# The head of a two-layer transformer kernel: tokens by lots of two tiles, query blocks by half the weights, and turns of the identity ahead

## The reference, cut to what matters

```
n  = layernorm(x)                          # x: (4, 256, 256)
q  = (n @ Wq + bq).reshape(b, 16, t, 128)  # Wq: (256, 2048)
h  = silu(n @ rw1.T + rb1)                 # router, hidden layer of 64
logits = (h @ rw2.T + rb2)[:, :16] + gates # top 2 of 16 experts, low-rank parts
```

## Time and profile before

| | us |
|---|---|
| median of 3 executions | 442.82 |
| lowest, highest | 442.76, 443.11 |
| the profiled execution, its time | 443.39 |
| its span, first to last instruction | 441.4 |
| PE busy in it | 422.6 |

### The profile page before, as it was taken

The page is one execution under the profiler, slowest core; times in us unless marked ns, Lnnn a source line. Parts: engine busy times, 40 slices in busy tenths (PEclk is TensorE's granted clock), DMA queues, the critical chain, the costliest instruction groups (busy, mean ns, idle before and its releaser), DMA issues.

```text
span 441.4 us, 8830 instructions
## 1 busy us (share of the span) xinstructions
PE 422.6 (96%) x3054; PEld 377.6 (86%) x3054; DVE 308.0 (70%) x906; ACT 245.7 (56%) x670; POOL 165.4 (37%) x293
## 2 busy tenths in 40 slices
PE   2999999899999999999999999999999989999897
PEld 1788889799999999999999999899998766577797
DVE  4645675678787888887877776657688985387442
ACT  3464563577777878786967686333314613553130
POOL 3050001455555555545555530101166005999000
PEclk9999999999999999999999999999999999999999
DMA  6920011141010100101000000000099932999002
GB/s 188 225 87 1 2 48 50 51 142 50 0 50 2 35 15 12 38 1 51 1 0 3 1 1 0 26 13 12 25 313 298 310 87 67 284 299 235 1 13 83
DMA packets 41979, 34.45 MB, mean 78 GB/s; under 512 B 6689, under 2 KB 40145, under 8 KB 41937
## 3 DMA queue, kind: packets, MB, share of 16 engines
q1 hardware_dynamic: 41552, 32.85, 26.5%
q0 software_dynamic: 384, 1.05, 0.8%
HBM read 31.80 MB, written 2.10 MB: 77 GB/s over the span
## 4 chain that ended last, share of the span: by engine, by line
PE 93%; DVE 3%; ACT 2%; issue 1%; DMA 1%; POOL 0%; DVEq 0%
PE bank L921 22%; PE bank L923 22%; PE bank L922 22%; PE bank L1079 5%; PE bank L1091 3%; PE bank L1070 3%; PE bank L1312 2%; PE bank L1279 2%; PE bank L1323 2%; PE bank L1324 2%; PE bank L1121 2%; PE bank L1299 2%; DVE GT L1787 1%; PE bank L1228 1%; DMA X<-in_L_attn_x 1%
## 5 line engine op out<-in xcount | busy, mean ns | idle before, releaser
L581 POOL TENSOR_TENSOR arena<-arena,rinv 128x384 f32<-128x384 f32 x64 | 53.0, 828 | 82.0 <-DVE rinv L1565 82.0
L921 PE MATMUL bank<-XTl,WA 128*128 128x512 f32 x128 | 54.3, 424 | 2.6 <-POOL WA L548 1.7
L923 PE MATMUL bank<-XTh,WA 128*128 128x512 f32 x128 | 51.3, 401 | 0.0
L922 PE MATMUL bank<-XTh,WA 128*128 128x512 f32 x128 | 51.3, 401 | 0.0
L746 ACT ACTIVATE PT<-bank 128x256 fp32r<-128x256 f32 x64 | 24.5, 382 | 34.1 <-PE bank L1079 34.1
L1569 DVE TENSOR_TENSOR PT<-bank,PT 128x256 fp32r<-128x256 f32 x64 | 27.2, 425 | 19.7 <-ACT arena L747 19.7
L921 PE MATMUL bank<-WA,XTh 128*128 128x256 f32 x128 | 38.4, 300 | 0.6 <-DVE K L1540 0.6
L572 POOL CAST Q<-arena 128x128 fp32r<-128x128 f32 x64 | 18.7, 292 | 48.4 <-PE bank L923 48.4
L922 PE MATMUL bank<-WA,XTl 128*128 128x256 f32 x128 | 35.7, 279 | 0.0
L923 PE MATMUL bank<-WA,XTh 128*128 128x256 f32 x128 | 35.7, 279 | 0.0
L1557 DVE CUSTOM_DVE_ANT_0 arena<-bank,posm 128x128 f32<-128x128 f32 x64 | 18.1, 282 | 20.9 <-PE bank L923 20.9
(11 more groups left out here) (327 smaller groups left out, 1449.8 us busy)
## 6 DMA issues: line engine op xcount, KB each, us to landing
arena<-in_L_ffn_Wg SPq DMA_DIRECT2D x6, 704.0 KB, 8.4
arena<-in_L_ffn_Wu SPq DMA_DIRECT2D x6, 704.0 KB, 10.5
arena<-in_L_ffn_Wd SPq DMA_DIRECT2D x6, 512.0 KB, 7.8
arena<-in_L_attn_Wq SPq DMA_DIRECT2D x4, 512.0 KB, 6.5
arena<-in_L_attn_Wk SPq DMA_DIRECT2D x8, 256.0 KB, 2.7
arena<-in_L_attn_Wv SPq DMA_DIRECT2D x8, 256.0 KB, 3.2
arena<-in_L_attn_Wo SPq DMA_DIRECT2D x1, 2048.0 KB, 8.6
arena<-in_L_ffn_Wd SPq DMA_DIRECT2D x6, 192.0 KB, 7.6
```

The lines of the kernel that those rows point to most:

```text
L581: pool.tensor_tensor(pr, pr, r[:, :, None].to_broadcast([P, 3, P]), ALU.mult).then_inc(s_p, 1)
L921: pe.matmul(dst, wh, xl, start=start, stop=False)
L922: pe.matmul(dst, wl, xh, start=False, stop=False)
L923: return pe.matmul(dst, wh, xh, start=False, stop=stop)
```

## The change

Ahead of everything PE turns the identity into bank 7, 32 times. Tokens are handled in four lots of two tiles instead of two of four: statistics, root, normalisation, turns (one bank for each lot, both halves of the features in it), high and low parts. The first two quarters of the query weights are loaded in halves and cut in halves; POOL makes both low halves of the first quarter. The first four blocks are computed by 256 tokens: `first_queries` does them for the first lot, one product of the three at a time over four banks, and `queries(0..3)` for the second lot. The blocks' order becomes that of `Q_AT`: quarter 0 half 0, quarter 1 half 0, quarter 0 half 1, quarter 1 half 1, then as before. `Q_FREE` gives the block after which a quarter's place is free. ScalarE's and VectorE's lists for the first 12 blocks are written out. The semaphores `s_wqa` and `s_w1` for the new halves are declared too.

```diff
+Q_AT = [(g, half, blk) for g, half in ((0, 0), (1, 0), (0, 1), (1, 1), (2, 0), (2, 1), (3, 0), (3, 1)) for blk in range(4)]
+Q_FREE = {2: 12, 3: 16, 4: 24, 5: 32}
+CHUNKS = 4
+WARM = 32
...
         @block.sync
         def _(sp):
-            for b in range(B):
+            def load_x(b):
                 sp.dma_start(X[:, 2 * b:2 * b + 2, :], x_t[:, b]).then_inc(s_x[b], 16)
-                if b == 1:
-                    sp.dma_start(WQv[:, 0], wq_t[:, :, 0:512]).then_inc(s_wq[0], 16)
+
+            def load_wq_halves(g):
+                for c in range(C):
+                    sp.dma_start(WQv[:, g, c], wq_t[:, c, 512 * g:512 * g + 512]).then_inc(s_wq[g] if c else s_wqa[g], 16)
+
+            load_x(0)
+            load_x(1)
+            load_wq_halves(0)
             for i, n in enumerate(("bq", "bk", "bv")):
                 sp.dma_start(VB[16 * i:16 * i + 16, :], row(a["L0_attn_" + n], H)).then_inc(s_vb, 16)
+            load_x(2)
+            load_x(3)
+            load_wq_halves(1)
             sp.dma_start(stR1, a["L0_ffn_rw1"]).then_inc(s_r, 16)
             sp.dma_start(stR2, a["L0_ffn_rw2"][0:E0, :]).then_inc(s_r, 16)
             sp.wait_ge(s_pad, 3)
             sp.dma_start(rb1c[0:HID, :], a["L0_ffn_rb1"].rearrange("(p a) -> p a", a=1)).then_inc(s_r, 16)
             sp.dma_start(rg[:, 0], a["L0_ffn_rb2"][0:E0].partition_broadcast(P)).then_inc(s_r, 16)
             sp.dma_start(rg[:, 1], a["L0_ffn_gates"].partition_broadcast(P)).then_inc(s_r, 16)
-            sp.dma_start(WQv[:, 1], wq_t[:, :, 512:1024]).then_inc(s_wq[1], 16)
             sp.dma_start(stW, two(a["L0_ffn_W"])).then_inc(s_sw, 16)
             sp.dma_start(stA, a["L0_ffn_A"].rearrange("(o e) r i -> (e r) o i", o=2)).then_inc(s_sw, 16)
...
             pool.wait_ge(s_w0, 1)
             pool.tensor_tensor(WA[:, 0, 1, 0:512], WQ[:, 0:512], WA[:, 0, 0, 0:512].bitcast(F32), ALU.subtract).then_inc(s_w0, 1)
+            pool.wait_ge(s_wh, 1)
+            pool.tensor_tensor(WA[:, 0, 1, 512:1024], WQ[:, 512:1024], WA[:, 0, 0, 512:1024].bitcast(F32), ALU.subtract).then_inc(s_wl, 1)
             pool.wait_ge(s_bo, 96)
...
-                    act.wait_ge(s_qf, 8 * (n - 1)) if n < 6 else act.wait_ge(s_kf, 8 * (n - 5))
+                    act.wait_ge(s_qf, Q_FREE[n]) if n < 6 else act.wait_ge(s_kf, 8 * (n - 5))
...
+            def deviations(i):
+                act.wait_ge(s_var, i + 1)
+                nc.scalar.activation(rstd[:, 2 * i:2 * i + 2], mv[:, 2 * i:2 * i + 2, 1], ACT.Sqrt).then_inc(s_std, 1)
+
+            def tokens_high(i):
+                act.wait_ge(s_xt, i + 1)
+                nc.scalar.activation(XTh[:, :, T * i:T * i + T], pb[4 + i][:].rearrange("p (c n) -> p c n", c=C), ACT.Copy).then_inc(s_xth, 1)
+
+            def first_high(g, c):
+                act.wait_ge(s_wq[g] if c else s_wqa[g], 16)
+                nc.scalar.activation(WA[:, g, 0, 512 * c:512 * c + 512], WQ[:, 1024 * g + 512 * c:1024 * g + 512 * c + 512],
+                                     ACT.Copy).then_inc(s_wh if c else (s_w0, s_w1)[g], 1)
...
+            deviations(0)
+            first_high(0, 0)
+            tokens_high(0)
+            deviations(1)
+            first_high(0, 1)
+            tokens_high(1)
+            first_high(1, 0)
+            deviations(2)
+            first_high(1, 1)
+            act.wait_ge(s_vc, 2)
+            q_copy(0)
+            deviations(3)
+            q_copy(2)
+            tokens_high(2)
+            q_copy(4)
+            tokens_high(3)
+            q_copy(6)
+            q_copy(8)
+            q_copy(10)
...
+            act.wait_ge(s_t, 2)
+            act.wait_ge(s_pad, 3)
+            nc.scalar.activation(R1Th[:, :, 0:HID], pb[5][:, 0:2 * HID].rearrange("p (c n) -> p c n", c=C), ACT.Copy).then_inc(s_tc, 1)
+            nc.scalar.activation(R2T[0:HID, :], pb[5][0:HID, 256:256 + E0], ACT.Copy).then_inc(s_tc, 1)
+            for g in range(1, 4):
...
-            def tokens_turn(f):
-                half, c = f // 2, f % 2
-                for i in range(4):
-                    j = 4 * half + i
-                    if c == 0:
-                        pe.wait_ge(s_xn, j + 1)
-                    ins = pe.transpose(pb[4 + f][:, P * i:P * i + P], XN[:, j, P * c:P * c + P], ident[:])
+            def tokens_turn(i):
+                if i == 2:
+                    pe.wait_ge(s_vc, 1)
+                for k in range(2):
+                    j = 2 * i + k
+                    pe.wait_ge(s_xn, j + 1)
+                    for c in range(C):
+                        ins = pe.transpose(pb[4 + i][:, T * c + P * k:T * c + P * k + P], XN[:, j, P * c:P * c + P], ident[:])
                 ins.then_inc(s_xt, 1)
...
+            def first_queries(i, c, part):
+                xs = slice(T * i, T * i + T)
+                for blk in range(4):
+                    wh, wl = (WA[:, 0, k].rearrange("p (c n) -> p c n", c=C)[:, c, P * blk:P * blk + P] for k in range(2))
+                    w, x = ((wh, XTh), (wh, XTl), (wl, XTh))[part]
+                    pe.matmul(pb[blk][:, xs], w, x[:, c, xs], start=(c == 0 and part == 0), stop=(c == C - 1 and part == 2))
...
-                g, half, blk = n // 8, n // 4 % 2, n % 4
-                if n == 0:
-                    pe.wait_ge(s_w0, 2)
-                else:
+                g, half, blk = Q_AT[n]
+                if n == 4:
+                    pe.wait_ge(s_w1, 2)
+                elif g >= 1:
                     pe.wait_ge(s_wh, g + 1)
                     pe.wait_ge(s_wl, g + 1)
...
+            for _ in range(WARM):
+                pe.transpose(pb[7][:, 0:P], ident[:], ident[:])
             tokens_turn(0)
+            pe.wait_ge(s_w0, 1)
+            pe.wait_ge(s_xth, 1)
+            first_queries(0, 0, 0)
+            pe.wait_ge(s_xtl, 1)
+            first_queries(0, 0, 1)
+            pe.wait_ge(s_w0, 2)
+            first_queries(0, 0, 2)
             tokens_turn(1)
-            queries(0)
-            queries(1)
-            queries(2)
+            pe.wait_ge(s_wh, 1)
+            first_queries(0, 1, 0)
+            first_queries(0, 1, 1)
+            pe.wait_ge(s_wl, 1)
+            first_queries(0, 1, 2)
+            pe.wait_ge(s_vb, 48)
+            pe.transpose(pb[6][:, 0:48], VB, ident[0:48, 0:48]).then_inc(s_t, 1)
+            for n in range(5):
+                queries(n)
             tokens_turn(2)
+            queries(5)
             tokens_turn(3)
-            pe.wait_ge(s_vb, 48)
-            pe.wait_ge(s_xtl, 1)
-            pe.transpose(pb[4][:, 0:48], VB, ident[0:48, 0:48]).then_inc(s_t, 1)
-            queries(3)
+            queries(6)
+            queries(7)
             router_turn()
-            for n in range(4, 8):
+            for n in range(8, 12):
                 queries(n)
             router_hidden()
-            for n in range(8, 16):
+            for n in range(12, 16):
...
+            def second_low(c):
+                if c == 0:
+                    dve.wait_ge(s_w1, 1)
+                else:
+                    dve.wait_ge(s_wh, 2)
+                    dve.wait_ge(s_wl, 1)
+                at = slice(512 * c, 512 * c + 512)
+                nc.vector.tensor_tensor(WA[:, 1, 1, at], WQ[:, 1024 + 512 * c:1536 + 512 * c], WA[:, 1, 0, at].bitcast(F32),
+                                        ALU.subtract).then_inc(s_wl if c else s_w1, 1)
...
             stats_of(0)
+            variances(0)
+            stats_of(1)
             norm(0)
+            variances(1)
             tokens_low(0)
+            norm(1)
+            stats_of(2)
             tokens_low(1)
-            dve.wait_ge(s_wh, 1)
-            nc.vector.tensor_tensor(WA[:, 0, 1, 512:1024], WQ[:, 512:1024], WA[:, 0, 0, 512:1024].bitcast(F32), ALU.subtract).then_inc(s_wl, 1)
-            stats_of(1)
-            norm(1)
             dve.wait_ge(s_t, 1)
-            nc.vector.tensor_copy(VC[:], pb[4][:, 0:48]).then_inc(s_vc, 1)
+            nc.vector.tensor_copy(VC[:], pb[6][:, 0:48]).then_inc(s_vc, 1)
             dve.wait_ge(s_vc, 1)
             nc.vector.tensor_scalar(bqs[:], VC[:, 0:H], SCALE, None, ALU.mult).then_inc(s_vc, 1)
+            variances(2)
+            second_low(0)
+            stats_of(3)
+            second_low(1)
+            variances(3)
+            norm(2)
+            q_copy(1)
+            norm(3)
             tokens_low(2)
+            q_copy(3)
             tokens_low(3)
+            q_copy(5)
+            q_copy(7)
+            q_copy(9)
...
+            q_copy(11)
+            dve.wait_ge(s_pad, 3)
+            weight_low(2, R1Tl[:, :, 0:HID], pb[5][:, 0:2 * HID].rearrange("p (c n) -> p c n", c=C), R1Th[:, :, 0:HID])
+            for g in range(1, 4):
+                w_low(g + 1, kvraw if g == 3 else wqraw(g + 1))
+                for n in range(8 * g + 1 + 4 * (g == 1), 8 * g + 8, 2):
```

(25 more changed lines are left out.)

84 lines of the change are left out of this document (27 added, 57 removed).

## The result

The changed kernel took 441.87 us (median of 11 executions, 440.99 to 442.28); the kernel before, run beside it, 443.57 (11 executions, 442.76 to 444.18). The ratio is 0.9962, 95% interval 0.9953 to 0.9971: a gain of 1.7 us where 3.0 was forecast. The time lies just above the range's upper end of 441.8.

The account below looks back on a forecast made before the run. PE bounds the kernel, busy 96% of the span. Turns to 7.1 + work 27.5 + waits 1.0, 0.5, 1.45 + allowance 0.1 put the logits at 37.65 against 40.66: gain 3.0, median 439.8 us, range 439.0 to 441.8.

Parts of the forecast that it names:

- rival A: Identity turns: the clock rises late, all 32 turns cold, ending at 8.4; gain 1.4, time 441.4; chance 0.15.
- B: Head: turning the identity does not raise the clock, which rises at 16.4; slower, 444.0; chance 0.05.
- wait for the router's low weights: Before the router's hidden layer: PE waits for VectorE's block 11 copy and subtraction, 1.45 us where nothing was waited for.
- the mark: Where query block 15 ends and the router's logits start: 40.66 before, forecast 37.65.
- rival E: Past the mark: the gain is taken back by something not seen; time 442.8; chance 0.07.
- C: ScalarE's weight copies: a weight half lands late; first half at 8.4 gives gain 1.7, 441.1; chance 0.10.
- the allowance of 0.1: Added to the sum for more changes between turns and products, 0.1 us that no single row gives.
- block 5's bank: Query block 5: held 0.5 us because VectorE's copy frees block 1's bank only at 17.0.
- Router turns and bias turn 0.45: PE's work up to the mark: these turns together take 0.45 us at the warm rate.
- Rows against: Rival D's counterargument: normalising 256 elements takes 0.41, about one a cycle, so no sign of a wider mode.
- rival D: Head: POOL's second low half blocks VectorE's normalisation; second tokens' turns 1.2 us late, gain 1.9, 440.9; chance 0.08.
- The handovers: Between engines throughout the new head: 0.05 us taken for each semaphore.

Follow-up runs that it names:

- number 7: The changed kernel with one load of 512 KB for each of the first two query weight quarters instead of two halves: 443.89 us, ratio 0.9977.
- number 10: The changed kernel with one load per weight quarter in place of two, a second time, beside the changed kernel: 444.45 us, ratio 0.9976.
- experiment 1: The changed kernel, but POOL's low part of the first weights' second half waits until tile 3 is normalised: 441.57 us, ratio 0.9953.
- experiment 14: The changed kernel with 24 turns, POOL's second subtraction later, router's copies earlier, and one extra identity turn behind each of blocks 8 to 15: 439.59 us, ratio 0.9914.
- experiment 4: The kernel before with the 32 identity turns ahead and nothing else: 441.45 us, ratio 0.9963.
- experiment 6: The changed kernel with the first four blocks done whole, by 512 tokens, lots of two tiles and turns kept: 447.36 us, ratio 1.0062.
- group 9 to 12: Four runs made together, with executions of the kernel before beside them, whose median is 445.00 us.
- number 9: The changed kernel itself again, unchanged, for a second profile beside its group's other runs: 444.15 us, ratio 0.9967.
- numbers 10, 11 and 12: The changed kernel with, in turn: one load per quarter, 0.9976; POOL's subtraction later and router's copies earlier without identity turns, 0.9947; the same with 24 turns, 0.991.
- group 1 to 4: Four runs made together, with executions of the kernel before beside them, whose median is 443.70 us.
- experiment 3: The changed kernel with POOL's second subtraction behind the norms and the router's copies earlier on ScalarE and VectorE: 439.82 us, ratio 0.9912.

## Why the prediction was half right

**Right.** The identity raises the clock, 4.2 us after the first turn (forecast 4.1), and the turns end at 7.15 (7.1): rivals A and B did not happen in this profile. That 4.1 was hit so closely is luck. In the other profiles with turns the rise came 2.7 to 5.9 us after the first one, and in numbers 7 and 10 (5.5 and 5.9) it is rival A's late rise; the last turn of the first tokens starts 0.64 and 0.86 later there than in the change, and number 7 gained 0.96 us where the change had gained 1.7. The wait for the router's low weights is there, released by VectorE, 1.41 us (1.45). PE bounds the rest, and the gain at the mark arrives at the end unchanged (400.7 us behind the mark in both), so rival E did not happen either. The products of 256 columns cost 0.118. The weight half was early enough (C) in the first profile, and 0.2 us late in the second. Of the 2.1 us by which the time missed, 0.75 is none of the mechanism's: the three executions that the forecast started from lay low among the eleven.

**Wrong: the sum to the mark,** 37.65 against 39.02. From the timeline above, a stretch's excess being its distance less 0.118, 0.2333 or 0.109 for each product or turn in it:

| term of the sum | forecast | measured | difference |
|---|---|---|---|
| identity turns end | 7.1 | 7.15 | 0.05 |
| wait ahead of the first product (7.15 to 8.53, less four turns) | 0.75 | 0.94 | 0.19 |
| wait for the low tokens (8.53 to 9.74, less eight products) | 0.25 | 0.27 | 0.02 |
| wait ahead of and inside the second lot's turns (9.74 to 11.09, less four products, four turns) | 0 | 0.44 | 0.44 |
| second lot's products up to the bias turn (11.09 to 12.68, less twelve), against the allowance of 0.1 | 0.1 | 0.17 | 0.07 |
| bias turn and router turns, with the distances beside them | 0.45 | 0.89 | 0.44 |
| block 5's bank | 0.5 | 0.51 | 0.01 |
| hidden layer's wait | 1.45 | 1.65 | 0.20 |
| other products and turns, the difference that is left | 27.05 | 27.00 | -0.05 |
| sum | 37.65 | 39.02 | 1.37 |

Three steps failed.

*"Router turns and bias turn 0.45."* They take 0.89, and the trace of before had most of it. Its PE timeline:

```profile
17.93 0.26 PE L994 MATMUL bank<-ident,arena 48*128 48x48 f32 x1
18.11 0.50 PE L921 MATMUL bank<-XTl,WA 128*128 128x512 f32 x1
18.45 0.40 PE L922 MATMUL bank<-XTh,WA 128*128 128x512 f32 x1
...
19.38 0.40 PE L923 MATMUL bank<-XTh,WA 128*128 128x512 f32 x1
19.71 0.33 PE L939 MATMUL bank<-ident,arena 64*128 64x64 f32 x2
19.97 0.20 PE L940 MATMUL bank<-ident,arena 16*64 16x16 f32 x1
```

The bias turn with the distances beside it took 0.29 there and takes 0.29 now, and from the end of the block ahead to the last router turn it is 0.36 in both. What follows that turn could not be read, because PE then waited for a bank until 21.03, and ScalarE's copy of block 0, not the turns, set that moment. So the router's turns cost the old kernel nothing and cost the new one 0.6 us. I built the new mark from nothing and compared it with a measured one, and so a term that was too small came out as a gain of 0.44.

*"Rows against" in rival D,* to which I gave 0.08. The sum has nothing between the first lot's products and the second lot's turns; there are 0.44 us. I argued that a normalisation at one element a cycle uses no wider mode and so can't be held. It is held: 1.62 us for two tiles under POOL's subtraction, 0.74 when POOL is moved away, and then the turns follow the products without a break (experiment 1). The Trainium skill, page "SBUF — State Buffer", section "Who interferes with whom", says that a tensor_scalar between SBUF tiles may take the port pair it shares with GpSimd, and that then one of them fully waits. The trace agrees in this: POOL began first, at 9.07, and VectorE, which began at 9.22, finished its first tile 0.16 us after POOL's end. The row on speed was no evidence against it. The rival's size was too large, 1.1 against a measured 0.5: it had both tiles normalised behind POOL's end, but the first of the pair was ready at 10.52, 0.16 after that end, and the second 0.32 later, and without the hold the turns start at 10.20, 0.2 later than forecast, since PE has the first lot's products until then.

*The handovers.* I took 0.05 for each semaphore. From the last turn's start at 7.48 ScalarE's copy started at 7.79, and from its end at 8.39 the product at 8.53: 0.31 and 0.14 where I had about 0.15 and 0.05. At the hidden layer's wait it is the same, 1.65 against 1.45: the last copy starts 0.2 us after the product that it waits for, and the product 0.15 after the subtraction. Besides, the distance behind the first product of a group that follows a wait or turns is 0.07 to 0.11 too long (8.53, 9.16, 11.09, 18.07, 30.55), and so is the one ahead of the bias turn (0.09). The groups at 9.74 and 12.12 begin behind a semaphore that had long been passed and show none of it, so that a semaphore by itself is not the reason. What is was not tried apart; experiment 14 only excludes the change between turns and products.

## What to carry to other kernels

Sum the differences between the two kernels, row against row, and not an absolute time against a measured one; whatever both share then drops out, mis-sized or not. What stood under a wait in the old kernel, as the router's turns did, and stands open in the new one goes in at its full price. Where an edit puts a VectorE tensor_scalar between SBUF tiles beside a POOL subtraction, write the sum with VectorE held until POOL ends, whatever its speed looks like alone. Feeding TensorE idle turns ahead of the first data pays only if no later wait lets the clock fall again: the turns and the finer pieces behind them are one edit. And look at the spread of a thing before giving it one value: the rise of the clock moved by 3.2 us between profiles.

## What the runs showed of the hardware

- The clock rose between 2.7 and 5.9 us after the first identity turn (at 4.33 and 7.52 in two of 13 profiles, the first turn at 1.58 or 1.59 in all of them). One execution gives a rise time that another does not repeat, and with 32 turns it moved the last turn of the first tokens from 6.78 to 8.34.
- It stayed up over waits of 0.78 and 1.41 us (the change) and 1.52, and fell behind waits of 2.12 (experiment 4, its profile) and 2.8 (experiment 6); each fall lasted 3.4 us. A pause near 2.1 us can go either way. In group 9 to 12 PE stands still at the same place, near 373 us, with no wait that the profile shows: for 2.13 in number 9, where the clock fell, and for 2.09, 2.09 and 2.07 in numbers 10, 11 and 12, where it did not. Stretches of number 9 around it read (length, busy us, PEclk third from the end):

```profile
372.00:376.30 4.30, 2.17 (x25) 0.99 (x28) 1.10 (x3) 0.59 (x2) 3.69 (x5) 1.00 0.41 114
376.40:379.80 3.40, 3.40 (x32) 1.28 (x24) 1.50 (x4) 1.22 (x5) 2.30 (x5) 0.50 1.04 314
```

  and PE's row behind the same pause in number 10:

```profile
376.71 0.33 PE L1342 MATMUL bank<-ident,arena 128*128 128x128 f32 x1 [2.09 <-issue]
```

  Executions with a mean clock of 0.996 were some 1.5 to 3 us longer than the others of the kernel before in group 9 to 12, six of 28, and one at 0.992; the sixteen of before in group 1 to 4 had none below 0.999.
- Ahead of the first rise the column PEclk reads 1.00 at the slow rate, while behind a fall it reads 0.50 at the same distance of 0.43 us (experiment 4). The distance between starts is the safer reading.
- VectorE's bn_stats were not held by POOL: two tiles took 0.74 from 9.85 in experiment 1, POOL subtracting from 10.08, and 0.74 alone. A tensor_scalar was. Which engine is held differs: later VectorE's subtraction of 1,024 columns took 1.73 us beside POOL's eight adds in the change and 1.23 beside the same adds in experiment 3, and the adds took 6.57 and 6.60, against 5.60 in the kernel before, where the subtraction came behind them and took 1.22. In experiment 1 it took 1.45.
